# The part stacks of two attention layers: one SBUF-to-SBUF DMA per block of sixteen partitions, in place of a trip through DRAM

## The reference, cut to what matters

```python
q = rope(rms_norm(x @ q_kernel)); k = rope(rms_norm(x @ k_kernel))     # layer 0
logits = einsum('btkgh,bskh->bkgts', q * scale, k)
probs = softmax(logits); encoded = einsum('bkgts,bskh->btkgh', probs, v)
...
qkv = x @ W_qkv.T + b_qkv                                              # layer 1
scores = where(causal, -inf, einsum('bnqd,bnkd->bnqk', q, k) * scale)
```

## Time and profile before

| | us |
|---|---|
| median of 3 runs (lowest, highest) | 854.34 (853.07, 855.31) |
| span of the profiled execution, first to last instruction | 851.4 |
| PE busy | 767.9 (90%) |
| DVE, ACT, POOL busy | 446.6, 359.7, 115.4 |
| mean granted PE clock | 0.970 of full speed |
| SP's DMA queue (q1), share of 16 engines | 27.0% |

### The profile page before, as it was taken

The page is one execution under the profiler, slowest core; times in us unless marked ns, Lnnn a source line. Parts: engine busy times, 40 slices in busy tenths (PEclk is TensorE's granted clock), DMA queues, the critical chain, the costliest instruction groups (busy, mean ns, idle before and its releaser), DMA issues. The chain is left out here.

```text
span 851.4 us, 11512 instructions
## 1 busy us (share of the span) xinstructions
PE 767.9 (90%) x3907; PEld 409.4 (48%) x3908; DVE 446.6 (52%) x1198; ACT 359.7 (42%) x565; POOL 115.4 (14%) x127
## 2 busy tenths in 40 slices
PE   5599999999999999999997879888998989989886
PEld 3222444444435556666665445434464445533675
DVE  2744554565435622222247676868765674662453
ACT  3389775685684012212223233444423442156030
POOL 0000000000000311111842411231011110022000
PEclk9699999999999999999999899989999999999999
DMA  7567207005107161111125870006300370000000
GB/s 217 148 204 223 93 26 209 27 25 149 38 26 247 43 198 46 43 45 46 32 84 169 251 201 2 1 27 187 110 1 3 106 216 1 2 1 26 14 12 26
DMA packets 51582, 75.01 MB, mean 88 GB/s; under 512 B 7607, under 2 KB 44763, under 8 KB 49227
## 3 DMA queue, kind: packets, MB, share of 16 engines
q1 hardware_dynamic: 49660, 69.26, 27.0%
q0 software_dynamic: 1872, 5.11, 2.2%
HBM read 46.57 MB, written 27.66 MB: 87 GB/s over the span
## 5 line engine op out<-in xcount | busy, mean ns | idle before, releaser
L656 PE MATMUL ps<-arena 128*128 128x256 f32 (+3 forms) x1084 | 326.7, 450 | 18.2 <-issue 2.9
L656 PEld LDWEIGHTS ps<-arena 128*128 128x128 f32 x1084 | 201.2, 195 | 106.6 <-issue 68.7
L970 ACT ACTIVATE arena<-ps 128x1024 f32<-128x1024 f32 x128 | 124.2, 1027 | 32.9 <-PE ps L711 32.6
L1067 ACT ACTIVATE arena<-ps 128x1024 f32<-128x1024 f32 (+3 forms) x128 | 82.9, 702 | 114.1 <-PE ps L903 114.0
L1450 DVE TENSOR_REDUCE arena<-ps 128x1 f32<-128x512 f32 (+3 forms) x176 | 100.4, 633 | 28.5 <-PE ps L881 27.6
L769 PE MATMUL ps<-arena 128*128 x184 | 86.5, 593 | 0.6 <-DVE arena L1177 0.6
L711 PE MATMUL ps<-arena 96*128 96x512 bf16 x256 | 71.4, 390 | 7.0 <-DMA arena<-q_stacks_dram 3.9
L1565 POOL TENSOR_SCALAR_AFFINE_SELECT arena<-arena 128x512 f32<-128x512 f32 x64 | 41.7, 652 | 253.3 <-ACT arena L1067 253.3
L725 PE MATMUL ps<-arena 128*32 128x512 f32 x512 | 69.6, 611 | 2.9 <-DVE arena L1223 2.7
L879 PE MATMUL ps<-arena 96*128 96x128 bf16 (+3 forms) x256 | 62.3, 303 | 9.6 <-DVE arena L1450 5.7
L648 PE MATMUL ps<-arena 128*128 128x128 f32 (+3 forms) x237 | 38.6, 302 | 23.3 <-DVE arena L1216 10.5
(11 more groups left out here) (153 smaller groups left out, 678.4 us busy)
## 6 DMA issues: line engine op xcount, KB each, us to landing
arena<-stacks_dram SPq DMA_DIRECT2D x16, 768.0 KB, 5.9
arena<-in_gate_up_proj SPq DMA_DIRECT2D x8, 1024.0 KB, 9.3
arena<-q_stacks_dram SPq DMA_DIRECT2D x8, 768.0 KB, 5.8
stacks_dram<-arena SPq DMA_DIRECT2D x16, 384.0 KB, 3.3
arena<-in_down_proj SPq DMA_DIRECT2D x8, 512.0 KB, 8.7
stacks_dram<-arena SPq DMA_DIRECT2D x16, 256.0 KB, 3.3
q_stacks_dram<-arena SPq DMA_DIRECT2D x8, 384.0 KB, 4.1
yg_dram<-arena SPq DMA_DIRECT2D x23, 128.0 KB, 1.7
```

The lines of the kernel that those rows point to most:

```text
L656: last = nc.tensor.matmul(dst[0:rows, lo:hi], a, w, start=(n == 0), stop=(n == len(pairs) - 1))
L970: nc.scalar.activation(probs[:, 2 * p:2 * p + 2, :], ps[:, 2 * p:2 * p + 2, :], ACT.Exp)\
L1067: nc.scalar.activation(cprobs[:, i % 2, 2 * p:2 * p + 2, P * kt:S], ps[:, 2 * p:2 * p + 2, P * kt:S], ACT.Exp).then_inc(exp_done[p], 1)
```

## The change

The DRAM scratch tensors go. A helper `stack_rows` issues six DMAs for a stack, one for each row block of sixteen partitions; each reads one part from the parts buffer (128 partitions x 512, or 64 x 512) and writes 16 partitions x 8 heads x 512 (or x 4), 128 KB (or 64 KB), in place. PE now waits for all 6 x 16 counts of a stack. ACT may overwrite a parts buffer when the six DMAs that read it have landed, that is, when the stack that they fill is complete.

```diff
+Q_PART = (0, 0, 0, 1, 1, 2)
+K_PART = (0, 1, 2, 0, 1, 0)
+STACKED = 16 * len(Q_PART)
...
-            def layer0_parts(b, i):
...
+            def stack_rows(stack, heads, part_of, part, done_sem):
+
+                for r in range(6):
+                    sp.dma_start(stack[HD * r:HD * (r + 1), heads, :], part[:, part_of[r], :]).then_inc(done_sem, 16)
 
             def layer0_stacks(b):
 
                 sp.wait_ge(parts_ready, 3 * b + 1)
-                layer0_parts(b, 0)
-                sp.wait_ge(parts_ready, 3 * b + 2)
-                layer0_parts(b, 1)
-                sp.wait_ge(s_scr[0], 96 * b + 48)
                 if b >= 2:
 
                     sp.wait_ge(pv_done, head0 * (b - 1))
...
+                stack_rows(k_stack[:, b % 2, :, :], slice(0, KV0), K_PART, parts[0:KV0 * HD, 0, :, :], s_stack[0])
+                for half in range(2):
+                    sp.wait_ge(parts_ready, 3 * b + 2 + half)
+                    stack_rows(q_stack[:, b % 2, :, :], slice(NH // 2 * half, NH // 2 * (half + 1)), Q_PART,
+                               parts[:, (half + 1) % 2, :, :], s_stack[1 + half])
...
                 if n == "cK":
                     half, of_k = i // 2, i % 2
                     sp.wait_ge(cparts_ready, 4 * b + i + 1)
...
+                    if b >= 2 and half == 0:
+
+                        sp.wait_ge(pv_done, head0 * B + headc * (b - 1))
+                    stack = (cq_stack, ck_stack)[of_k]
+                    stack_rows(stack[:, b % 2, :, :], slice(NH // 2 * half, NH // 2 * (half + 1)), (Q_PART, K_PART)[of_k],
+                               cparts[:, of_k, :, :], cs_stack[of_k][half])
...
                     if i == 0:
-                        pe.wait_ge(s_stack[b % 2], 32 * (b // 2 + 1))
+                        pe.wait_ge(s_stack[0], STACKED * (b + 1))
+                        pe.wait_ge(s_stack[1], STACKED * (b + 1))
...
                     if 3 * b + i >= 2:
-                        act.wait_ge(s_scr[i % 2], 96 * b if i == 0 else 48 * b if i == 1 else 96 * b + 48)
+                        act.wait_ge(s_stack[(2, 1, 0)[i]], STACKED * (b + 1 if i == 2 else b))
...
                     if 4 * b + i >= 2:
-                        act.wait_ge(cs_scr[i % 2], 48 * ((4 * b + i) // 2))
+                        act.wait_ge(cs_stack[i % 2][1 - i // 2], STACKED * (b + i // 2))
```

More of the change, by code:

```diff
@@ L372, in post_ln_layers @@
         parts_ready = sem("parts_ready")
-        s_scr = [sem(f"parts_in_dram{i}") for i in range(2)]
-        s_stack = [sem(f"stacks_loaded{i}") for i in range(2)]
-        s_stack2 = [sem(f"last_q_stacks_loaded{i}") for i in range(2)]
+        s_stack = [sem(f"stack_loaded_{name}") for name in ("k", "q0", "q1")]
         s_full = [sem(f"scores_full{i}") for i in range(2)]
@@ L413, in post_ln_layers @@
         cparts_ready = sem("cparts_ready")
-        cs_scr = [sem(f"cparts_in_dram{i}") for i in range(2)]
-        cs_stack = [[sem(f"cstacks_loaded{h}{i}") for i in range(2)] for h in range(2)]
+        cs_stack = [[sem(f"cstack_loaded_{name}{h}") for h in range(2)] for name in ("q", "k")]
         m_parts = sem("max_parts_ready")
@@ L610, in _ @@
                     sp.wait_ge(cparts_ready, 4 * b + i + 1)
[L611 to L622, removed]
-                        for t, dst in ((0, cq_stack), (1, ck_stack)):
-                            sp.wait_ge(cs_scr[t], 48 * (2 * b + half + 1))
-                            sp.dma_start(dst[0:STACK, b % 2, NH // 2 * half:NH // 2 * (half + 1), :],
-                                         cscr[b, t, half].rearrange("r (d h) n -> (r d) h n", d=HD))\
-                              .then_inc(cs_stack[half][b % 2], 16)
+                    if b >= 2 and half == 0:
[3 more added lines that the diff above has]
+                               cparts[:, of_k, :, :], cs_stack[of_k][half])
                 elif n == "cM":
@@ L874, in _ @@
                     if i % (len(MAXES) // 2) == 0:
-                        pe.wait_ge(cs_stack[h0 // (NH // 2)][b % 2], 32 * (b // 2 + 1))
+                        for of_k in range(2):
+                            pe.wait_ge(cs_stack[of_k][h0 // (NH // 2)], STACKED * (b + 1))
                     dst = take(pe, step)
```

5 lines of the change are left out of this document (1 added, 4 removed).

## The result

| | us |
|---|---|
| before, median of 4 runs beside it | 854.83 |
| changed kernel, median of 4 runs (lowest, highest) | 884.91 (881.96, 887.0) |
| ratio, 95% interval | 1.0348 (1.032 to 1.0377) |
| profiled execution, span | 880.2 (before 851.4) |

What follows compares the result with a forecast made beforehand. PE, busy 90% of the span, was taken as the bound, with ACT's parts-buffer waits exposed. The terms -2.1 + 2.6 + 7.0 + 6.8 gave 14.3 us slower than 854.34: 868.6 us, range 857 to 877.

Steps and rivals of the forecast that it cites:

- three cases: Lanes into sixteen neighbouring partitions: one per pair (0.53 us a DMA), per four (1.06, taken) or per eight (2.1).
- the signs that I had named: Wu0 7 us later; 1 KB pieces 100 to 150 ns; cQ3 waits 7 or more; L684 wait under 2, later.
- place 5: Layer 1, samples 2 and 3: ACT waits 3.7 us longer for k half 0; loss 3.4 us twice, 6.8.
- The price of a stack, 7.7 us: An 8-head stack lands 7.7 us after its parts are ready: 1.15 + 6.0 for six DMAs + 0.5 tail.
- a lane absorbs some at first: Six DMAs of a stack: lanes take some bytes at first, so 6.0 us was counted instead of 6.3.
- place 3: Opening of layer 1: ACT's cQ3 waits 7.4 us longer for k half 0, and everything moves; loss 7.0 us.
- place 1: Opening of layer 0: q's stack lands sooner, attention starts at 38.5 instead of 40.57; 2.1 us gained.
- PE's first maxima need half 0 alone: Opening of layer 1: four stacks queue up, but the first maxima come behind all these steps; no further loss counted.
- Place 2: Layer 0: sample 1 nothing; samples 2 and 3, ACT waits 5.3 us instead of 3.75; loss 1.3 twice, 2.6.
- my cases: Four lanes 868.6 us (0.55); issue pitch alone 859.0 (0.24); faster 851 (0.06); fewer lanes 907 (0.07); cancelling, about 854 (0.08).
- sample 1: Layer 1, place 4: ACT's waits grow by 3 to 4 us, covered by its later 5.42 us wait for PE.

Runs made afterwards that it cites:

- lanes: The stack DMAs alone, without the kernel's computation, in 12 forms: six queued into sixteen neighbouring partitions landed in 8.2 us, with partitions 6 apart in 5.6.
- strided: Changed kernel with row r of a head at partitions r, r+6, ... instead of sixteen neighbours: 862.23 us, ratio to before 1.0106.
- filler3: Changed kernel with one extra matmul call before cN1 and one before cH0 in layer 1's samples 2 and 3: 882.48 us, ratio to before 1.0346.
- filler2: Changed kernel with ten extra matmuls (three before cN1, two before cH0 per block), meant for layer 1's samples 2 and 3: 889.36 us, ratio to before 1.0403.

## Why the prediction was wrong

Right: the mechanism and its sign. The exposed resource was the parts buffer, not the stack. The DMA of 1.06 us and the 124 GB/s measured 1.04 us and 126 GB/s; of these, two rows of a constant's load gave the rate of one lane, while the number of lanes, four, was picked as the middle of three cases, and that it came out is in part luck. The Trainium skill ("SBUF — State Buffer", section "Door 1: The DMA port swizzle") gives sixteen neighbouring partitions four ports, four partitions to a port, with 104 GB/s measured; the forms of lanes agree with the ports, and the rate measured here, 126 GB/s, is higher. Of the signs that I had named, a 1 KB piece took 130 ns (1.04 us for the eight pieces that each engine has in a DMA; 100 to 150 forecast), and Wu0 came 8.6 us later relative to the steps before the opening (7 forecast). PE's wait at L684 was 2.55 us, not under 2, and attention did not start later (40.37, before 40.57). ACT's wait at cQ3 in samples 2 and 3 was 5.5 and 5.1 us, not 7: its copy before had already waited 4.2 and 4.5. The forecast was a sum of waits of 14.3 us, and PE's idle time grew by 15.6; that the two are near is luck. By the ledger below 22.9 us of the lag are not in cH's matmuls, and for some 7.3 of them PE was not idle but busy longer, as in the sixteen matmuls of cV.

Wrong, step by step.

1. **The step that failed: place 5, "Loss 3.4 us twice ... 6.8".** It measured 7.9 + 7.8, 8.9 of the 14.5 us that the sum fell short. Two terms. The wait up to cH is 4.9, not 3.4: k's parts were ready at 597.29 (DVE's L1399) and ACT went on at 606.24, 8.95 us later, for which I had 7.7; before it was 4.03, and the difference of 4.9 reached PE whole. The 0.3 us of slack was gone; ACT's copy before it, at 598.09, now waited too (4.16 us; before, at 580.93, only 0.15 us, and for PE), and PE waited for the exponentials behind it (L877, 1.07 us). And 3.0 us a sample come from eight matmuls at the half clock. No term of the sum was for the clock, though the trace of before already showed it below full speed where PE idles (0.83 in the opening of layer 1). 5.9 of the 14.5 missing us are this.
2. **The price of a stack, 7.7 us.** 8.7 in the opening of layer 1, 8.3 and 8.95 in sample 2; alone 8.2. I took off 0.3 because "a lane absorbs some at first" and put 0.5 for the tail. One DMA alone lands in 3.0 us, and five more at 1.04 make 8.2: nothing is absorbed. This is 0.5 to 1.25 us in every exposed place of layer 1. It is the larger part of the 1.8 us by which place 3 fell short, and of what place 1 lacked, where the gain was 1.0 us instead of 2.1: attention started at 40.37, with 0.8 us of lag that this execution brought from its first loads.
3. **"PE's first maxima need half 0 alone", the end of place 3.** True, but behind them stood another user of the queue, which I had not priced: the two 16 KB DMAs of the maxima (L604; L632 before) landed in 4.3 us instead of 2.2, behind the stack DMAs that had not landed yet, and PE's first scores of layer 1 waited 3.64 us instead of 1.57: 2.0 us. In strided, where the stacks land sooner, L604 took at most 2.1 again. L604's landings in the changed kernel:

```profile
DMA to landing us min/median/max: 2.1/2.1/4.3
```

4. **Place 2, 1.3 us twice.** 1.1 and 1.8: the sum was right, 2.9 for 2.6. k's stack took 5.5 us, for which I had 5.3; in sample 2 more slack took up some of it (0.7, for which I had 0.2), in sample 3 none did: the matmul that needs ACT's evacuation behind the copy (L698 <- ACT L951) waited 2.03 us, before 0.26.

The range ended at 877 because my cases all varied the landing time and shared one conversion, a wait on ACT costs PE as much as its length. What the half clock adds behind the waits is in none of them.

How the 28.8 us divide, then: 14.3 as foreseen; 3.0 and 1.8 more in waits at places 5 and 3; 2.5 in layer 0, of which 0.8 came with this execution's first loads and 1.1 is the later landing; 2.0 from the maxima's DMAs; 5.9 from the half clock in samples 2 and 3; less 0.7 in sample 1. The 5.9 are read from two places of the trace; filler3 bears them out in its trace alone, since no variant gave them back in full. Open is where sample 1's 0.7 us come from, and what in the idle pattern decides that the clock falls in one execution and not in another.

## What to carry to other kernels

Before shortening a transfer, ask which of its two ends is waited for: the result or the release of the source. Here a source buffer was released by the quickest part of the old way, and any new way had to beat that part, not the whole; a third buffer (26.8 us) was worth at least as much as the faster transfer (22.7). When a DMA touches few partitions, look at which ones: the same bytes in the same packets to spaced partitions were worth 22.7 us. And when waits grow in stretches where PE is otherwise the bound, reckon with its half clock behind them: here 3 us for eight matmuls, twice. Where PE had to wait at the next step anyway, it cost nothing.

## What I had not expected of the hardware

- Reading from sixteen neighbouring partitions is as slow as writing to them (3.0 us for 128 KB either way). Writing to partitions 4 or 8 apart takes 2.3, and a step of only 2 brings nearly all of it back (2.4). Spaced reading was not measured.
- In lanes a DMA within SBUF costs SP's queue 507 to 602 ns (medians of the eight forms), a DMA of the same size between SBUF and DRAM 303 to 320. In the kernels the gap is smaller: 600 ns for a stack DMA, 490 for a parts write of before in layer 1 (medians). Six issues within SBUF are 3.3 to 3.6 us, most of the old wait.
- DMA share and bytes part ways: in the opening of layer 1 the share was 0.84 at 108 GB/s, before 0.79 at 225. The share can be packets that stand in line for a few partitions: with the partitions spaced, and the same bytes, a stack's six DMAs landed in 5.6 us instead of 8.2.
- The same instructions fell to the half clock at different places in two profiled executions: the sixteen matmuls of cV in sample 2 took 5.22 us in the changed kernel, 3.62 in filler2 (whose extra matmuls come later). Filler2's PE then waited 2.38 us for ACT instead of 0.93 and went on at 607.72, the changed kernel's at 608.05.
